# Three bf16 attentions of a transformer stack rewritten as float32r flows whose operands are laid out by DMA

## The chip, the cores and the metric

The kernel runs on one core of one Trainium2 chip, as one launch. The metric is the device time of that launch in microseconds (us). The engines are named as the profile names them: PE is TensorE (its weight loads are listed apart as PEld), DVE is VectorE, ACT is ScalarE, POOL is GpSimd, and SP is SyncE, which here issues nearly all DMA transfers.

## The reference, cut to what matters

Eight sub-layers follow each other on an activation of shape (8, 256, 128), each added to it through a tanh gate:

```python
x = x + jnp.tanh(g_xattn[0]) * _L0_xattn_ref(_layernorm(x), ctx_1024, ctx_1024)
x = x + jnp.tanh(g_ffn[0])   * _L0_ffn_ref(_layernorm(x), ...)
x = x + jnp.tanh(g_xattn[1]) * _L1_xattn_ref(...)
x = x + jnp.tanh(g_ffn[1])   * _L1_ffn_ref(...)
x = x + jnp.tanh(g_xattn[2]) * _L2_xattn_ref(_layernorm(x), ctx_1024, ctx_1024, W, b, mask)
x = x + jnp.tanh(g_ffn[2])   * _L2_ffn_ref(...)
x = x + jnp.tanh(g_xattn[3]) * _L3_xattn_ref(...)
x = x + jnp.tanh(g_ffn[3])   * _L3_ffn_ref(...)
```

The change touches four attentions. Three have 16 heads of 8 channels over 8 sequences of 256 queries and 256 keys: L0's (rotary, causal), L2's (causal, with a padding mask) and L3's (with four projections, not causal). The fourth lies in L0's feed-forward: a chain of six nodes, each with an attention of 8 heads of 16 channels over the same 8 sequences, 48 attentions in all, here called L0f. Each is `softmax(q k^T * scale) v` in float32.

## The kernel before, in words

**Precision.** A float32 value is too fine for one fast matmul pass, so each operand is cut into parts. The three small-head attentions use class `Heads`: POOL (`att_pool`, lines 359 to 400) cuts each of q and k into three bf16 parts and writes six products' worth of them side by side (six times 8 columns for each head), so that a contraction over 48 rows gives the product in full. L0f uses class `Flow`: two parts (high and low) in float32r, three products, 48 rows for its heads of 16 channels.

**Small-head flow (`att_pool`, `att_pe`, `att_act`, `att_dve`).** One unit is one sequence: 16 heads, worked in 8 pairs. PE turns the stacked bf16 parts by transposes (events K and T, 16 of 128x128 each; line 434). ACT copies the turned q out of PSUM (552), DVE the turned k (566). Pass A (476) gives the scores with queries on the rows; DVE takes each row's maximum from them (573, 574, or 576 where not causal), writes its negative into the stack (586, 588), and PE turns the q stack once more with this row in it (event X, 16 transposes; ACT copies it at 556). Pass B (489) computes the scores again with keys on the rows and the maximum already subtracted. ACT takes the exponential (548), V (503) multiplies by the values with a column of ones that yields the denominator, O (543) copies the sum out, R (513) turns it back, and DVE divides (598, 601). In the causal layers two groups of four mask matmuls (444 and 453) come before A and B of each pair.

**L0f's flow (`flow_*`).** One unit is one node and sequence: 8 heads, 4 pairs. Matmuls with the node's weights (event S, line 952) already leave q and k transposed in PSUM. ACT writes the high parts to `Z` (1049), DVE the low parts (event L, 1097). Then SP copies, from SBUF to SBUF, six pieces of 128 KB into `QK` (event D, line 876), each piece spreading one pair of parts into every third row of a slot. `QK` is a ring of three units. The negated maxima are turned by PE (event N, 979), negated by DVE into `NMrow` (1091), and SP copies them as one row into the slots (866). Pass B (990) of the first two pairs waits for the first such copy, of the last two for the second.

**Order.** Every engine walks the same list, `events()`, and executes its own kinds in that order. Software pipelining is in that list: in one step, pass B of one unit runs with pass A of the next, while units further on are prepared. SP walks it too, in order, so a DMA behind a waiting DMA waits with it. PE executes in order; A of a pair waits until DVE has taken the maxima of the pair before (one set of PSUM banks), B until ACT has taken the exponential of the pair before.

**Around it.** Each stage begins and ends with a barrier of all five engines (line 259 is that wait in the profile). Before a small-head flow POOL clears the two stacks and V (350 to 356) and does stage work: in L0 it rotates k, in L2 it turns the padding mask into numbers (1791). Before L0f's flow POOL blanks the ring (1159).

Of the kernel before, what the change touches and what calls it, by code (L numbers as in the profile page):

```python
# [8 lines left out]
F32 = mybir.dt.float32  # L9
# [12 lines left out]
PARTS = 6  # L22
MASKED = -1.0e30
ROUND = 12582912.0
Q_SLOTS = ((0, 3), (3, 2), (5, 1))


class Heads:


    def __init__(self, dh, causal):
        self.dh, self.causal = dh, causal
        self.H = D // dh
        self.halves = self.H // 8
        self.units = 8
        self.per = self.H // self.units
        self.cols = P // self.per
        self.pad = PARTS * dh
        self.top = self.pad + 1
        self.end = self.pad + 3  # L40
        self.scale = float(dh) ** -0.5
        self.pairs = self.H // 2

    def events(self):

        pairs, last = self.pairs, self.halves - 1
        out = [("K", 0, 0), ("K", 0, 1), ("T", 0, 0), ("T", 0, 1)]
        for s in range(B + 1):  # L50
            a, b, more = s < B, s >= 1, s + 1 < B
            for j in range(pairs):
                if j == pairs - 1 and more:
                    out += [("K", s + 1, 0), ("K", s + 1, 1)]
                if a:
                    out.append(("A", s, j))
                if j < pairs - 1 and b:
                    out.append(("B", s - 1, j + 1))
                elif j == pairs - 1 and a:
                    out.append(("B", s, 0))  # L60
                if b and j % 2 == 1:
                    out.append(("V", s - 1, j // 2))
                    if j % 4 == 3:
                        out.append(("O", s - 1, j // 4))
                if b and j == 0:
                    out.append(("X", s - 1, 1))
                if a and j == pairs // 2:
                    out.append(("X", s, 0))
                if j == 1 and s >= 2:
                    out.append(("R", s - 2, last))  # L70
                if b and last and j == 5:
                    out.append(("R", s - 1, 0))
                if j == pairs - 2 and more:
                    out += [("T", s + 1, 0), ("T", s + 1, 1)]
        return out + [("R", B - 1, last)]


class Flow:
# [6 lines left out]
    def __init__(self, dh, causal, units, node):  # L85
        self.dh, self.causal, self.units, self.node = dh, causal, units, node
# [6 lines left out]
        self.scale = float(dh) ** -0.5  # L93

# [10 lines left out]
    def events(self):  # L105
# [10 lines left out]
        for s in range(-3, self.units + 1):  # L116
            z, w, a, b, f = s + 3, s + 2, s + 1, s, s - 1
            for j in range(self.pairs):
                if ok(b):
                    out.append(("B", b, j))  # L120
                if ok(a):
                    out.append(("A", a, j))
                if j == 2 and ok(z):
                    out.append(("L", z, 0))
                if j == 0 and ok(b):
                    out.append(("N", b, 1))
                if j == half and ok(a):
# [15 lines left out]
                if j == 1 and ok(z):  # L143
                    out.append(("S", z, 0))
# [12 lines left out]
def flamingo(nc, T, out):  # L157
    with ExitStack() as ctx:
# [30 lines left out]
        Mx = sb("Mx", [P, 2, 16])  # L189
        Rden = sb("Rden", [P, 2, 16])  # L190
# [6 lines left out]
        sh = ExitStack()  # L197
        Qst = sb("Qst", [P, 2, 2, 8, P], BF16, scope=sh)
        Kst = sb("Kst", [P, 2, 8, P], BF16, scope=sh)
        QT = sb("QT", [P, 2, 8, S], BF16, scope=sh)  # L200
        KT = sb("KT", [P, 2, 8, S], BF16, scope=sh)
        QpT = sb("QpT", [P, 8, S], BF16, scope=sh)
# [5 lines left out]
        rope = sb("rope", [P, 2, 2, 4], scope=s0)  # L208
        s0.close()
# [5 lines left out]
        padi = sb("padi", [P, NT], I32, scope=s4)  # L215
        padf = sb("padf", [P, NT], scope=s4)
        s4.close()
        sh.close()
# [8 lines left out]
        q_split, k_split = sem("q_split"), sem("k_split")  # L227
        tpT_full, tpT_free = sem("tpT_full"), sem("tpT_free")
        tpK_full, tpK_free = sem("tpK_full"), sem("tpK_free")
        tpX_full, tpX_free = sem("tpX_full"), sem("tpX_free")  # L230
        sm_full, max_done, max_in = sem("sm_full"), sem("max_done"), sem("max_in")
# [108 lines left out]
        def stack(ap, L):  # L340

            return ap.rearrange("p t u (g c) -> p (t u g) c", g=L.per)

# [3 lines left out]
        def stack_fill(g, L, pad_bias=None):  # L347

            e = g.eng
            g.link(e.memset(Qst[:], 0.0))  # L350
            g.link(e.memset(Kst[:], 0.0))
            g.link(e.memset(V[:, 0:NT * L.H * 32], 0.0))
            g.link(e.memset(v_view(L)[:, :, :, L.dh:L.dh + 1], 1.0))
            for t in range(2):
                g.link(e.memset(stack(Qst[:, t], L)[:, :, L.pad:L.pad + 1], 1.0))
            g.link(e.memset(stack(Kst[:], L)[:, :, L.top:L.end], 1.0))
# [2058 lines left out]
```

## Time and profile before

| what | value |
|---|---|
| median of 3 runs | 2091.3 us (2089.96 to 2099.73) |
| the profiled execution | 2090.75 us |
| its span, first to last instruction | 2088.8 us |
| mean granted clock of TensorE | 0.857 of full |
| busy: PE, DVE, ACT, POOL | 1383.4, 1399.1, 806.9, 448.6 us |
| flow of L0's attention, about | 52 to 218 us |
| L0f's flow, about | 263 to 774 us |
| flow of L2's attention, about | 1325 to 1489 us |
| flow of L3's attention, about | 1608 to 1779 us |

A row of a timeline reads: start in us, duration in us, engine, line, operation, written and read tile, shapes, count, and in brackets how long the engine had been idle and what ended that. A row of a group reads: busy us, mean ns of one, then the idle time in front of the group and its cause. Matmul durations contain a pipeline latency of about 0.17 us, so four matmuls that follow each other overlap in the rows; the start of the next group tells how long they occupy PE.

### The profile page before, as it was taken

How to read it: one execution, taken by the hardware profiler on the slowest of the kernel's cores; microseconds unless marked ns; L12 is line 12 of the kernel's file. 1: busy time of each engine (PE TensorE's matmuls, PEld its weight loads, DVE VectorE, ACT ScalarE, POOL GpSimd, SP SyncE). 2: the span in 40 equal slices, each digit the busy share in tenths (PEclk: the TensorE clock that was granted, in tenths of full speed). 3: DMA queues.
4: the chain of work that ended last, by engine and by line, in shares of the span. 5: the costliest groups of instructions: out<-in, count | busy, mean ns of one | idle time of the engine just before them, and what ended most of it. 6: DMA issues, size and time to landing. Idle time of an engine off the chain costs nothing. (4 is left out here: it accounts for less than half of the span.)

```text
span 2088.8 us, 34728 instructions
## 1 busy us (share of the span) xinstructions
PE 1383.4 (66%) x13753; PEld 966.7 (46%) x13754; DVE 1399.1 (67%) x2126; ACT 806.9 (39%) x1151; POOL 448.6 (21%) x596
## 2 busy tenths in 40 slices
PE   0788168888888870788888833388523677140898
PEld 0565146566656640465665521266413344120797
DVE  5565446676667758577677768566586676859565
ACT  0466136666666650333333311266320477010110
POOL 6431332222222101122222200532003331000221
PEclk9999569999999995999999965599856699655798
DMA  2011322233222311000000000000000000110242
GB/s 66 3 9 10 91 64 78 79 86 79 78 78 80 90 32 62 1 1 1 1 1 1 1 11 12 12 2 2 11 0 30 1 2 2 59 20 0 86 131 94
DMA packets 97736, 76.51 MB, mean 37 GB/s; under 512 B 42612, under 2 KB 84148, under 8 KB 96692
## 3 DMA queue, kind: packets, MB, share of 16 engines
q1 hardware_dynamic: 96564, 73.10, 12.8%
q8 instruction: 107, 1.75, 0.4%
q0 software_dynamic: 1024, 1.32, 0.3%
q14 instruction: 41, 0.34, 0.1%
HBM read 33.10 MB, written 3.15 MB: 17 GB/s over the span
## 5 line engine op out<-in xcount | busy, mean ns | idle before, releaser
L1086 DVE TENSOR_REDUCE Mf<-bank 128x4 f32<-128x1024 f32 x192 | 234.5, 1221 | 148.6 <-PE bank L972 148.4
L1039 ACT ACTIVATE Pt<-bank 128x1024 f32<-128x1024 f32 x192 | 196.8, 1025 | 83.5 <-PE bank L990 82.8
L548 ACT ACTIVATE Pt<-bank 128x768 f32<-128x768 f32 (+1 forms) x192 | 169.4, 882 | 135.4 <-PE bank L489 134.5
L1312 POOL TENSOR_TENSOR Psum<-Pt 128x512 f32<-128x512 f32 x64 | 81.1, 1267 | 315.3 <-ACT Pt L1431 315.3
L990 PE MATMUL bank<-QK 50*128 50x256 f32 x768 | 98.9, 336 | 51.0 <-DMA QK<-NMrow 50.0
L758 PE MATMUL bank<-ident,Qf 128*128 128x128 f32 x64 | 14.3, 416 | 156.9 <-SPq L259 94.5
L1479 DVE RECIPROCAL st<-bank 128x256 f32<-128x256 f32 x64 | 111.9, 1748 | 6.9 <-PE bank L1392 6.8
L896 POOL CAST parts<-nodes 128x256 fp32r<-128x256 f32 x96 | 38.2, 397 | 339.1 <-PE bank L952 339.1
L1454 DVE TENSOR_TENSOR qk_lo<-bank,qk_hi 128x512 fp32r<-128x512 f32 x64 | 44.1, 689 | 97.1 <-ACT qk_hi L1423 97.1
L990 PEld LDWEIGHTS bank<-QK 50*128 50x128 f32 x768 | 58.8, 190 | 106.9 <-DMA QK<-NMrow 59.2
L573 DVE TENSOR_REDUCE Mx<-bank 128x2 f32<-128x256 f32 x128 | 54.3, 424 | 80.5 <-PE bank L476 76.4
L1003 PE MATMUL bank<-Pt,V 128*32 128x256 f32 x1536 | 107.8, 400 | 0.1
L1431 ACT ACTIVATE Pt<-bank 128x1024 f32<-128x1024 f32 x64 | 65.5, 1024 | 77.8 <-PE bank L1375 77.8
L503 PE MATMUL bank<-Pt,V 128*32 128x256 f32 (+1 forms) x1536 | 91.7, 357 | 2.9 <-ACT Pt L548 2.9
L476 PE MATMUL bank<-KT,QT 49*128 49x256 bf16 (+1 forms) x768 | 73.6, 273 | 30.0 <-DVE Mx L576 26.6
L576 DVE TENSOR_REDUCE Mx<-bank 128x4 f32<-128x1024 f32 x64 | 78.2, 1221 | 21.9 <-PE bank L476 21.8
L1968 POOL DMA_INDIRECT xg<-s_rows,sloti x32 | 29.3, 916 | 293.0 <-PEq L259 201.1
L972 PE MATMUL bank<-QK 49*128 49x256 f32 x768 | 81.9, 292 | 12.1 <-DMA QK<-Z 6.8
L574 DVE TENSOR_REDUCE Mx<-bank 128x2 f32<-128x512 f32 x128 | 87.0, 680 | 0.0
L758 PEld LDWEIGHTS bank<-ident,Qf 128*128 128x128 f32 x64 | 12.9, 224 | 157.7 <-SPq L259 95.0
L434 PE MATMUL bank<-identb,Kst 128*128 128x128 bf16 x384 | 33.0, 241 | 76.8 <-POOL Kst L387 69.0
L1387 PE MATMUL bank<-Pt,V 128*64 128x256 f32 x512 | 70.2, 395 | 19.5 <-DVE AnT L1481 19.5
(367 smaller groups left out, 3687.6 us busy)
## 6 DMA issues: line engine op xcount, KB each, us to landing
QK<-Z SPq DMA_DIRECT2D x288, 128.0 KB, 3.3
Wup<-in_L_upT SPq DMA_DIRECT2D x16, 512.0 KB, 3.5
Wdn<-in_L_downT SPq DMA_DIRECT2D x16, 256.0 KB, 3.7
Aup<-in_L_aupT SPq DMA_DIRECT2D x16, 128.0 KB, 3.5
QK<-NMrow SPq DMA_DIRECT2D x96, 4.0 KB
WeT<-in_L_WeT SPq DMA_DIRECT2D x1, 1280.0 KB
s_rows<-XG SPq DMA_DIRECT2D x1, 1032.0 KB, 8.2
tA<-in_x_heads SPq DMA_DIRECT2D x1, 1024.0 KB
```

What stands on the lines that cost most here:

```text
L476: last = pe.matmul(bank[x][:, t * S:t * S + w], QT[rs, n % 2, u, t * P:(t + 1) * P], KT[rs, n % 2, u, 0:w], start=(not L.causal and t == 0 ...
L503: last = pe.matmul(bank[4][32 * x:32 * x + 32, c + q0:c + S], Va[:, 2 * n + k, 4 * i + x, :], Pp[:, (f + x // 2) % 4, x % 2, k * S:k * S + ...
L548: act.activation(Pp[:, g % 4, :, 0:w], banks[:, 2:4, 0:w], ACT.Exp, scale=L.scale).then_inc(exp_done, 1)
L574: d.tensor_reduce(Mx[:, 1, hs], banks[:, 0:2, S:2 * S], AX, ALU.max).then_inc(max_done, 1)
L576: d.tensor_reduce(Mx[:, :, hs].rearrange("p t h -> p h t"), banks[:, 0:2, :].rearrange("p h (t k) -> p h t k", t=2), AX, ALU.max).then_inc ...
L972: last = pe.matmul(bank[x][:, t * S:(t + 1) * S], QK[rs, u % 3, k, 0, t * P:(t + 1) * P], QK[rs, u % 3, k, 1, :], start=(t == 0), stop=Tru ...
L990: last = pe.matmul(bank[2 + x][:, t * S:(t + 1) * S], QK[rs, u % 3, k, 1, t * P:(t + 1) * P], QK[rs, u % 3, k, 0, :], start=(t == 0), stop ...
L1003: last = pe.matmul(bank[4][32 * x:32 * x + 32, S * (j % 2):S * (j % 2) + S], Va[:, 2 * n + k, 4 * j + x, :], Pp[:, (f + x // 2) % 4, x % 2 ...
L1039: act.activation(Pp[:, g % 4], banks[:, 2:4, :], ACT.Exp, scale=L.scale).then_inc(exp_done, 1)
L1086: d.tensor_reduce(m, banks[:, 0:2, :].rearrange("p h (t k) -> p h t k", t=2), AX, ALU.max).then_inc(max_done, 1)
L1312: e.tensor_tensor(Psum[:, q % 2], Pp[:, q % 4, :, 0:S], Pp[:, q % 4, :, S:2 * S], ALU.add).then_inc(key_sum, 1)
L1479: d.reciprocal(st1[:], y[:, S:2 * S]).then_inc(pair_done, 1)
```

## The change

`Heads` and `att_*` go; all four attentions are `Flow`s. What is different for the three with 8 channels:

- Two float32r parts instead of three bf16 ones: 24 rows of products, one for the mask and one for the maximum, in slots of 32 rows, four heads to a column block of 128 rows.
- POOL only reorders columns: four copies of 128x128 to a unit (event S). PE turns them with 4 float32 transposes, ACT copies the high parts (128x512), DVE subtracts for the low parts (128x512).
- SP lays the parts into the slots: per unit 12 copies of 64 KB (events D, 0 to 3, three copies each), in L2 a 13th with the padding mask. Two small copies per unit bring the maxima.
- In a step, A stands ahead of B, as before in the causal layers. D stands at pairs 1, 2, 3 and 5, the maxima (N) at pairs 0 and 4, S at pair 7, L at pair 0. R is at pairs 1 and 5, V at pairs 0, 2, 4 and 6.
- The masks stay as they were, bf16, four matmuls each. The short matmuls of the causal layers (128 columns) become float32r too.
- POOL clears only V, then blanks the ring with six casts of 128x1024; in L2 the mask is now handled as 16 x 2048 numbers rather than 128 x 16. SP also stores L0's output rows from within the flow, at event R.

For L0f:

- the ring holds four units instead of three, so blanking takes eight casts instead of six;
- the six copies of a unit go in two lots of three: the first at pair 3 of the step in which its parts are made, the second at pair 1 of the next step. Before, all six stood at pair 0 of the next step.

The core of the diff:

```diff
-        self.copies = 3 * self.per
+        self.copies = 3 * self.per + padded
+        self.ring = 4 if node else 3
...
             for j in range(self.pairs):
-                if ok(b):
+                if ok(b) and self.node:
                     out.append(("B", b, j))
                 if ok(a):
                     out.append(("A", a, j))
-                if j == 2 and ok(z):
+                if ok(b) and not self.node:
+                    out.append(("B", b, j))
+                if self.node and j == 2 and ok(z):
                     out.append(("L", z, 0))
+                elif not self.node and j == 0 and ok(w):
+                    out.append(("L", w, 0))
...
-                if j == 0 and ok(w):
-                    out.append(("D", w, 0))
+                if self.node and j == 3 and ok(z):
+                    out.append(("D", z, 0))
+                elif self.node and j == 1 and ok(w):
+                    out.append(("D", w, 1))
+                elif not self.node and j in (1, 2, 3, 5) and ok(w):
+                    out.append(("D", w, j - 1 - j // 5))
...
-                if j == 1 and ok(z):
+                if j == (1 if self.node else self.pairs - 1) and ok(z):
                     out.append(("S", z, 0))
...
+        def slots_blank(g, L):
+            for r in range(L.ring):
+                for k in range(2):
+                    g.eng.tensor_copy(L.QK[:, r, :, k, :], bc(L.rowk[:, k:k + 1].unsqueeze(1), [P, 4, S]))
...
+                elif kind == "R" and rows_out and j == L.outs - 1:
+                    rows_out(u)
                 elif kind == "D":
-                    e.wait_ge(stk_done, u + 1)
-                    if u >= 3:
-                        e.wait_ge(st_full, base["P"] + L.pairs * (u - 2))
-                    for r in range(L.per):
-                        rows = slice(L.slot * r, L.slot * r + 4 * L.dh)
+                    e.wait_ge(L.stk_done, u + 1)
+                    if u >= L.ring:
+                        e.wait_ge(st_full, base["P"] + L.pairs * (u - L.ring + 1))
+                    if L.padded and j == 0:
+                        e.dma_start(L.QK[L.pad:P:L.slot, u % L.ring, :, 1, :].bitcast(F32),
+                                    padr[:, u, :].bitcast(F32)).then_inc(L.slots_in[u % L.ring], 16)
+                    rows = slice(L.slot * j, L.slot * j + 4 * L.dh)
+                    for f, pick in enumerate((slice(1, 3), slice(1, 4, 2), slice(0, 3, 2))):
...
+                if kind == "S" and not L.node:
+                    for k, src in enumerate((Qf, Kf)):
+                        for t in range(2):
+                            e.tensor_copy(L.permuted(L.order[:, u % 2, k, t, :], out=True),
+                                          L.permuted(src[:, 2 * u + t, :])).then_inc(L.parts_in, 1)
...
+                    else:
+                        last = act.copy(L.Z[:, u % 2, 1:3, :].rearrange("p k s -> p (k s)"), b)
...
+                    else:
+                        last = d.tensor_tensor(L.Z[:, u % 2, 0:4:3, :], b.rearrange("p (k s) -> p k s", k=2),
+                                               L.Z[:, u % 2, 1:3, :].bitcast(F32), ALU.subtract)
...
-                (wx[:, 3], T["L2_WT"]), (bx[:, 3], row_bc("L2_xattn_b", D)), (padi[:], T["pad_cols"])]
+                        (padi[:], T["mask_BxS2_if0"].unsqueeze(0).to_broadcast([16, B, S])),
...
-                g.link(g.eng.tensor_scalar(padf[:], padi[:], 1.0, MASKED, ALU.is_equal, ALU.mult))
+                g.link(g.eng.tensor_scalar(padr[:], padi[:], 1.0, MASKED, ALU.is_equal, ALU.mult))
```

## Rows read from the trace of the kernel before

**Rows 1.** Stretch of L0f's flow: busy PE, PEld, DVE, ACT, POOL; clock, DMA.

```profile
277.00:770.00 493.00, 427.03 (x4258) 292.59 (x4258) 331.62 (x504) 312.96 (x483) 100.22 (x186) 0.96 0.29 77
```

**Rows 2.** Timeline of L0's small-head flow, one pair to the next.

```profile
143.41 0.40 PE L444 MATMUL bank<-cmask,identb 128*128 128x128 bf16 x4 [0.40 <-DVE Mx L574]
...
143.96 0.34 PE L476 MATMUL bank<-KT,QT 49*128 49x128 bf16 x4
...
144.39 0.86 PE L503 MATMUL bank<-Pt,V 128*32 128x256 f32 x16
...
144.68 0.68 DVE L574 TENSOR_REDUCE Mx<-bank 128x2 f32<-128x512 f32 x1
...
145.68 0.39 PE L444 MATMUL bank<-cmask,identb 128*128 128x128 bf16 x4
```

**Rows 3.** The same timeline, mask of the pair after.

```profile
148.99 0.39 PE L444 MATMUL bank<-cmask,identb 128*128 128x128 bf16 x4
```

**Rows 4.** Groups by line and shape; then two rows of L0f's timeline.

```profile
L972 PEld LDWEIGHTS bank<-QK 49*128 49x128 f32 x768 | 61.7, 194 | 15.5 <-DMA QK<-Z 7.8 <-issue 3.9 <-DVE Mf L1086 3.2
L961 PE MATMUL bank<-Kf,nodes 128*128 128x128 f32 x192 | 30.3, 282 | 0.0
L476 PEld LDWEIGHTS bank<-KT,QT 49*128 49x128 bf16 x768 | 22.6, 96 | 63.1 <-DVE Mx L576 33.6 <-issue 13.5 <-ACT QT L552 3.6
...
504.82 0.51 PE L990 MATMUL bank<-QK 50*128 50x256 f32 x4
...
505.16 0.40 PE L972 MATMUL bank<-QK 49*128 49x256 f32 x4
```

**Rows 5.** Waits of PE in L0f; then the timeline around two `NMrow` copies.

```profile
PE bank L990 <- DMA QK<-NMrow: 50.0, 44, 2.4
...
285.56 5.13 SPq L866 DMA_DIRECT2D QK<-NMrow  x2
...
287.32 0.79 PE L990 MATMUL bank<-QK 50*128 50x256 f32 x4 [0.89 <-DMA QK<-NMrow]
...
510.10 5.36 SPq L866 DMA_DIRECT2D QK<-NMrow  x2
...
512.55 0.50 PE L990 MATMUL bank<-QK 50*128 50x256 f32 x4 [1.14 <-DMA QK<-NMrow]
```

**Rows 6.** Timeline of two flow starts: L0's small heads, then L0f.

```profile
51.69 0.40 POOL L378 CAST Kst<-Kf 128x256 bf16<-128x256 f32 x1 [8.16 <-DVEq L259]
...
60.92 0.50 PE L476 MATMUL bank<-KT,QT 49*128 49x128 bf16 x4 [0.79 <-ACT QT L552]
...
267.40 2.93 PE L952 MATMUL bank<-parts,wst 128*128 128x256 f32 x12 [2.13 <-DVE bv L1125]
...
270.92 7.84 SPq L876 DMA_DIRECT2D QK<-Z  x12
...
277.94 0.80 PE L972 MATMUL bank<-QK 49*128 49x256 f32 x4 [6.76 <-DMA QK<-Z]
```

**Rows 7.** POOL: three groups, then its timeline in L2 and L3.

```profile
L350 POOL MEMSET Qst<- 128x4096 bf16 x3 | 10.5, 3512 | 54.0 <-DVEq L259 54.0
L1159 POOL CAST QK<-rowk 128x1024 fp32r<-128x1024 f32 x6 | 7.5, 1294 | 8.2 <-DMA V<-in_L_ffn_We 8.2
L886 POOL COPY Kf<-V 128x128 f32<-128x128 f32 x12 | 4.5, 404 | 4.8 <-PEq L259 4.8
...
1324.37 0.32 POOL L1791 TENSOR_SCALAR padf<-padi 128x16 f32<-128x16 int32 x1 [7.01 <-issue]
...
1616.43 0.66 POOL L380 TENSOR_TENSOR rest<-Kf,Kst 128x256 f32<-128x256 f32 x1 [7.80 <-issue]
```

**Rows 8.** L3's maxima: their group; one unit apart on the timeline.

```profile
L576 DVE TENSOR_REDUCE Mx<-bank 128x4 f32<-128x1024 f32 x64 | 78.2, 1221 | 21.9 <-PE bank L476 21.8
...
1697.56 0.60 DVE L586 TENSOR_SCALAR Qst<-Mx 128x16 bf16<-128x16 f32 x1
...
1714.83 0.60 DVE L586 TENSOR_SCALAR Qst<-Mx 128x16 bf16<-128x16 f32 x1
```

More of the change, by code:

```diff
@@ L21, with __init__ @@
 NT = B * S // P
-PARTS = 6
 MASKED = -1.0e30
 ROUND = 12582912.0
[L25 to L75, printed above, removed]
 class Flow:
-    def __init__(self, dh, causal, units, node):
-        self.dh, self.causal, self.units, self.node = dh, causal, units, node
+    def __init__(self, name, dh, causal, units, node=False, padded=False):
+        self.name, self.dh, self.causal, self.units = name, dh, causal, units
+        self.node, self.padded = node, padded
         self.H = D // dh
@@ L208, in flamingo @@
         rope = sb("rope", [P, 2, 2, 4], scope=s0)
+        L0.hold(sb, s0)
         s0.close()
@@ L471, in att_pe @@
                         pe.wait_ge(max_done, g)
                     for t in range(2):
-                        w = P if (L.causal and t == 0) else S
+                        w = P if L.causal and t == 0 else S
                         for x in range(2):
-                            rs, u = rows(2 * i + x, L.pad + 1)
-                            last = pe.matmul(bank[x][:, t * S:t * S + w], QT[rs, n % 2, u, t * P:(t + 1) * P],
-                                             KT[rs, n % 2, u, 0:w], start=(not L.causal and t == 0),
+                            rs, k = L.rows(2 * j + x, L.top)
+                            last = pe.matmul(bank[x][:, t * S:t * S + w],
+                                             L.QK[rs, u % L.ring, k, 0, t * P:(t + 1) * P],
+                                             L.QK[rs, u % L.ring, k, 1, 0:w], start=(not L.causal and t == 0),
@@ L484, in att_pe @@
                         pe.wait_ge(exp_done, g)
                     for t in range(2):
-                        q0 = P if (L.causal and t == 1) else 0
+                        q0 = P if L.causal and t == 1 else 0
                         for x in range(2):
-                            rs, u = rows(2 * i + x, L.end)
-                            last = pe.matmul(bank[2 + x][:, t * S:t * S + S - q0], KT[rs, n % 2, u, t * P:(t + 1) * P],
-                                             QpT[rs, u, q0:S], start=(not L.causal and t == 0), stop=True,
-                                             skip_group_check=True)
+                            rs, k = L.rows(2 * j + x, L.top + 1)
+                            last = pe.matmul(bank[2 + x][:, t * S:t * S + S - q0],
+                                             L.QK[rs, u % L.ring, k, 1, t * P:(t + 1) * P],
+                                             L.QK[rs, u % L.ring, k, 0, q0:S], start=(not L.causal and t == 0),
+                                             stop=True, skip_group_check=True)
@@ L500, in att_pe @@
+                    o = Ub + L.outs * u + j // 2
+                    if j % 2 == 0 and o > 0:
+                        pe.wait_ge(ot_free, o)
                     for k in range(2):
-                        q0 = P if (L.causal and k == 1) else 0
+                        q0 = P if L.causal and k == 1 else 0
+                        o = S * (j % 2)
                         for x in range(4):
-                            last = pe.matmul(bank[4][32 * x:32 * x + 32, c + q0:c + S], Va[:, 2 * n + k, 4 * i + x, :],
+                            last = pe.matmul(bank[4][32 * x:32 * x + 32, o + q0:o + S], Va[:, 2 * n + k, 4 * j + x, :],
@@ L529, in turn_bank @@
[L529 to L544 removed]
+                    b = turning(kind, u, j)
@@ new lines, in flow_pe @@
+                    pe.wait_ge(norm_done, 2 * (Ub + u + 1))
+                    for t in range(2):
+                        last = pe.transpose(b[:, t * P:(t + 1) * P], O[:, 2 * n + t, :], ident[:, :])
+                    last.then_inc(t_full, 1)
+                elif kind == "U":
+                    b = turning(kind, u, j)
+                    pe.matmul(b[:, 0:S], WeS[:, c, :], nodes[:, c, cols], start=True, stop=False)
+                    pe.wait_ge(t_done, u + 1)
+                    pe.matmul(b[:, 0:S], Wn[:, 3, c, :], attT[:, u % 2, :], start=False, stop=True).then_inc(u_full, 1)
```

774 lines of the change are left out of this document (291 added, 483 removed).

## The prediction

> **What bounds the kernel now.** I first split the span into stages and ask each flow what ends last in it. In L0f's flow, 493 us long, PE is busy 427.03 us at a granted clock of 0.96 (nearly all of it at 2.4 GHz) and every other engine less [rows 1]. PE runs almost back to back there, except for one wait: the table of waits gives 50.0 us in 44 times to the copy of `NMrow` [rows 5]. That is where L0f can be shortened. The small-head flows are bound by a loop, not by a busy engine: mask matmuls, pass A, the maxima on DVE, the next masks. In rows 2 the mask starts at 143.41, A 0.55 later, and DVE's second reduction ends at 144.68 + 0.68 = 145.36; with 0.06 for the signal the next mask could start at 145.42, a turn of 2.01 us. It started at 145.68, so this turn took 2.27: V and the turning of the sums (R) were still in PE's queue. The turn after it takes 148.99 − 145.68 = 3.31 [rows 2, 3], since the 32 transposes of K and T and their copies are in it. A unit is eight turns: five of 2.01, two of 2.27 and one of 3.31 make 17.9 us. L3, without masks, takes 1714.83 − 1697.56 = 17.27 a unit [rows 8].
>
> **Part 1, L0f's copies in two lots.** Of a row copy issued when nothing else is under way, the reader starts 287.32 − 285.56 = 1.76 us later; of one issued right behind six 128 KB copies, 512.55 − 510.10 = 2.45 us later [rows 5]. I take the difference, 0.69 us, as the price of standing behind them. After the change three copies leave after the second row copy of a step and three after the first, so the row copy at pair 2 follows only three copies that ended some 2.3 us earlier, and the one at pair 0 three that ended about 2 us earlier. I take 1.76 for both: 44 × 0.69 = 30 us less over the 48 units. Ends: nothing, if what is late is the copy's own latency; 50 us if the whole wait goes. What is late next is PE itself, at 87% of this stretch. Blanking takes two more casts, of 1.29 us on average and less where DVE doesn't disturb them [rows 7]; POOL is the last engine at that barrier, so nothing hides them: +2. L0f: −28.
>
> **Part 2, start of a small-head flow.** Before, the first A begins 60.92 − 51.69 = 9.2 us after POOL starts [rows 6]. Now: POOL's four reorderings 4 × 0.40 = 1.6 [rows 7]; then transposes, ACT's and DVE's copies, which in L0f took 270.92 − 267.40 = 3.5 from PE's start to the first DMA [rows 6], with more matmuls, so 3.0 here. SP's 12 issues took 7.84, or 0.65 each [rows 6], so the last starts 7.2 after the first. From the start of the sixth issue (270.92 + 5 × 0.65) to the A that waits for it is 277.94 − 274.17 = 3.8; for pieces of half the size I take 3.0. Sum 14.8, or +5.6; POOL's reorderings overlap a little, so I take +5, in L2 +5.6 with the 13th copy. Bounds: +3 (all but the issues a third shorter) and +9 (a piece that takes twice as long to land).
>
> **Part 3, a turn of the causal flows.** A float32r weight load is 194 ns on average, a bf16 one 96 [rows 4], and it stands open between the masks and A: +0.09. Four float32r matmuls of 256 columns occupy PE 505.16 − 504.82 = 0.34 [rows 4]; two by two, at 2.4 GHz, they would stream in 0.21, so 0.13 of each group is weight load, of which I take +0.11 as new. No row shows a float32r matmul of 128 columns. Low end: it streams at the rate of 256 columns, +0. High end: as plain float32 of 128 columns, 282 ns, about 0.11 of it beyond the 0.17 of latency, where bf16 takes half: +0.05 per group [rows 4]. That row has its size and word width, so I take it. The loop grows to 2.01 + 0.09 + 0.05, and 0.03 for the second weight load, 2.18. PE's own work in a turn with V: mask to A 0.55 + 0.09; A and B 0.43 up to V [rows 2] + 2 × 0.16; V 0.8 (its 0.86 less the tail): 2.19, with N 0.2 more. A unit: 8 × 2.18 + 0.45 = 17.9. What the longer turns take, the 48 transposes that go give back; the four big copies that ACT loses lay beside the loop. Steady pace: no change, from −0.5 (low end) to +1.4 a unit (a turn 0.2 longer, V slots bound by PE). Seven units with A and B together: −4 to +10 in each of L0 and L2. The eight turns with A alone, at half clock, and the last eight with B alone carry the same additions: 8 × 0.17 + 8 × 0.12 = +2.3.
>
> **Part 4, POOL before the flows.** It loses two fills, 3.5 [rows 7] and half of that, and gains six casts (7.5, with one stalled), about +1. In L0 DVE was last (POOL had waited 8.16 us at the end [rows 6]), so +0.5 for the later DMA. In L2 POOL is the last too: +1, and the mask conversion, 16 numbers in 0.32 before, becomes 2048 in a row; a cast of 1024 takes 1.29, so 2.3 more; casts beside DVE's long layer norm add another 1.2. L2: +4.5, from 0 to +9. The stall of 7.01 in front of it stays [rows 7]. In L3 the stall of 7.80 stood in front of POOL's first TENSOR_TENSOR after a barrier that had everything else waiting [rows 7]; now POOL has only copies and casts there, before which no row shows such a stall: −7.8.
>
> The Trainium skill (GPSIMD Engine Reference, Instruction dispatch) says that the first call of a freshly loaded kernel costs some 6 us more. The two stalls of 7.0 and 7.8 agree in size; both come behind a partition reduction. If that rule held for copies as well, the first cast or fill would pay it; in L2 that would be under the layer norm and give 7 us back, in L3 it would change nothing, and the sum would be 7 less.
>
> **Part 5, L3's pace.** DVE needs 1.22 for a maximum [rows 8]; a turn is A 0.45, DVE 1.22, 0.06: 1.74. PE with V: 0.34 + 0.34 + 0.2 + about 1.07 (0.86 and the columns that the causal layers leave out), 1.95, and with N 2.3; DVE at pair 0 also has the low parts and a row, 2.4. The unit: 2.4 + 1.9 + 1.95 + 1.74 + 2.3 + 1.9 + 1.95 + 1.74 = 15.9, −1.4 against 17.27 [rows 8], ×7 = −9.6. Flows start at half clock (four matmuls of A take 0.80 in rows 6, 0.40 in rows 4), and there V fills a turn alone, so I take −8. Start: +5 of part 2, −7.8 of part 4, ends +1.8. L3: −9, from −22 to +2.
>
> **Sum.** L0: 0.5 + 5 + 2.3 + 0 = +8. L0f: −28. L2: 4.5 + 5.6 + 2.3 = +12.4. L3: −9. Together −16.6 on the profiled execution's 2090.75 (span 2088.8 and 1.95 around it), which lies 0.6 below the median of 2091.3. So 2074, −0.8%. Half a percent (10.5 us) is about what can be told from no change.
>
> The Trainium skill (DMA: Bandwidth & Descriptors, Why a DMA increments its semaphore by 16 and not by 1) says that a copy is spread over the largest number of engines up to 16 that divides the outermost sizes of both sides. By it a piece that ends in 8 rows runs on 8 engines, where L0f's of 16 rows had 16; it would occupy them as long as the old ones did theirs. A DMA share of 0.29 [rows 1] of some 10 us a unit is 2.9 us for six copies, or 0.48 a piece, under the 0.65 of an issue, and the sum stays; the rule makes the rival of the copies below possible. No row here shows how many engines a copy had.
>
> **Rivals.**
> (a) L0f's wait does not move: the row copy needs 2.4 us whatever stands before it, because its end must be signalled behind all data of its queue. For it: the wait is there in 44 of 48 units [rows 5]. Against it: 1.76 at the flow's start [rows 5], though at a time when PE ran at half clock. The small heads then stand alone: 2074 + 28 = 2102, slower than before. It decides from 17 us of lost gain. Chance 0.14.
> (b) Causal turns cost more: short float32r matmuls are dearer than plain float32, or the PE queue with A, B, V and N is longer than the loop. For it: my sum for a V turn is already at 2.19 of 2.18. 14 units × 1.4 = +20: 2094, no change. Chance 0.20.
> (c) The wait in L0f goes altogether, and L2's stall hides: 2074 − 20 − 7, about 2047 to 2055. For it: shortening the chain also lets DVE start earlier. Chance 0.16.
> (d) The slot copies bound the small heads: 12 copies a unit, SP occupied 12 × 0.65 + two rows + two stores, 10.3 of 17.9. It decides from 1.4 us a copy; at 1.6 a unit takes 20, and 14 × 2.1 + 7 × 4.1 = 58 more give 2132. Against it: L0f moves as many bytes in 10 us [rows 1]. Chance 0.07.
> The forecast itself has 0.43, with 2062 to 2086.
>
> **The numbers.** Faster by over 0.5% (under 2080): most of the forecast, all of (c), a little of (b): 0.57. Within: most of (b), the rest of the forecast, some of (a): 0.25. Slower: most of (a), (d), tail of (b): 0.18. Range 2048 to 2101, which leaves out (d) and half of (a) above and the best of (c) below; the likeliest case's own is 2062 to 2086.
>
> **What would show it.** In the changed trace: PE's wait for `NMrow` in L0f near 20 us instead of 50, and units some 0.6 us shorter; between POOL's first reordering and the first A about 14.8 us, three times; turns of 2.18 in the causal flows, and the float32r matmuls of 128 columns near 282 ns; POOL's stall still in L2, none in L3; L3's units near 16. It is wrong if a unit of the causal flows is over 19 us, or if L0f's stretch stays at 493 us.

## The result, and the profile after

| | before | after |
|---|---|---|
| median | 2095.5 us (4 runs) | 2217.4 us (4 runs, 2195.0 to 2228.9) |
| ratio | | 1.0548, 95% interval 1.0454 to 1.0641: slower |
| profiled execution, span | 2088.8 us | 2193.1 us |
| mean granted clock of TensorE | 0.857 | 0.792 |
| busy: PE, DVE, ACT, POOL | 1383.4, 1399.1, 806.9, 448.6 us | 1505.3, 1379.5, 732.5, 364.0 us |

The slowest run of the changed kernel, 2228.9 us, lies over 1.5% above its fastest and is not in the ratio; the other three have a median of 2211.6 us, and every difference from the changed kernel below is counted from that. The forecast of 2074 was wrong by 143 us (138 from 2211.6), outside its range and on the other side. DVE, ACT and POOL have less to do than before; PE is busy 122 us longer though 48 transposes a unit are gone. To see where, I cut both spans at marks that both kernels have: DVE's negated row maxima in L0f (96 of them), and POOL's first instruction in L2's and in L3's flow. Of a tile's row the columns are the duration (ns, minimum/median/maximum), then the first and last start; under it stand rows of the timeline. Before:

```profile
L1091 DVE TENSOR_SCALAR NMrow<-bank x96: 401/402/412, 285.1 to 763.0; 4x256 fp32r<-4x256 f32 x96
```

```profile
1324.87 0.40 POOL L378 CAST Kst<-Kf 128x256 bf16<-128x256 f32 x1 [0.19 <-SPq L259]
...
1607.67 0.40 POOL L378 CAST Kst<-Kf 128x256 bf16<-128x256 f32 x1 [20.53 <-SPq L259]
```

After, with POOL's two other rows that matter for the starts:

```profile
L638 DVE TENSOR_SCALAR l0f_NMrow<-bank x96: 401/402/411, 327.6 to 765.3; 4x256 fp32r<-4x256 f32 x96
```

```profile
34.76 1.03 POOL L730 TENSOR_TENSOR tB<-ctxS,rope 128x512 f32<-128x512 f32 x1 [7.56 <-issue]
...
1328.07 7.13 POOL L1576 TENSOR_SCALAR padr<-padi 16x2048 fp32r<-16x2048 int32 x1 [7.32 <-issue]
1335.39 0.73 POOL L376 COPY l2x_order<-Qf 128x128 f32<-128x128 f32 x2 [0.19 <-POOLq L236]
...
1673.42 0.73 POOL L376 COPY l2x_order<-Qf 128x128 f32<-128x128 f32 x2 [21.12 <-DVEq L236]
```

| stretch | before | after | after − before |
|---|---|---|---|
| start to L0f's first row (with L0's flow) | 285.1 | 327.6 | +42.5 |
| L0f, first to last row | 477.9 | 437.7 | −40.2 |
| to POOL's start in L2 | 561.9 | 570.1 | +8.2 |
| L2's start to L3's start | 282.8 | 338.0 | +55.2 |
| L3's start to the end | 481.1 | 519.7 | +38.6 |

L0f gained more than forecast, and the three small-head flows lost about 33 (L0), 51 (L2) and 48 us (L3) beside what was counted for them. Why is in the stretches of L2's and L3's flow. The columns are the stretch and its length, busy us (and instructions) of PE, PEld, DVE, ACT and POOL, the granted clock, the DMA share and GB/s. Before, L2 in full pace, then L3:

```profile
1400.00:1475.00 75.00, 64.22 (x1033) 45.88 (x1030) 49.31 (x110) 46.73 (x58) 17.96 (x30) 1.00 0.01 2
1680.00:1763.00 83.00, 62.38 (x872) 36.62 (x872) 65.16 (x88) 61.95 (x68) 21.23 (x34) 1.00 0.01 1
```

After, L2, then L3, then for comparison L0f:

```profile
1400.00:1450.00 50.00, 44.39 (x526) 31.74 (x524) 25.59 (x57) 20.59 (x28) 2.87 (x8) 0.84 0.13 46
1450.00:1500.00 50.00, 48.39 (x390) 35.18 (x390) 19.68 (x43) 15.08 (x20) 0.00 (x0) 0.50 0.10 34
1705.00:1882.00 177.00, 163.20 (x1117) 93.82 (x1118) 86.03 (x110) 80.05 (x88) 5.54 (x16) 0.50 0.08 28
360.00:770.00 410.00, 380.80 (x3958) 263.55 (x3958) 305.34 (x464) 290.25 (x449) 90.81 (x168) 1.00 0.31 84
```

The clock column is the finding: 0.50, the lower of TensorE's two levels (1.2 GHz), through all of L3's flow and parts of L2's, with PE busy 163.20 / 177 = 92% of L3's stretch; before, 1.00 with PE busy 75 to 86%. So it was not want of busy time that kept the engine at half clock; since at half rate the same work fills more of the time, the comparison that decides is e2's, below, with the same instructions. The durations say the same: a causal group of A takes 0.49 us at full rate and 0.79 at half. (In L0 the column prints 1.00 where A takes 0.79; there the durations count.) The timeline shows one such fall in L2. From 1440 to 1447 us PE was busy 5.55 of 7 us (79%) at a clock of 1.00, and its longest pause was 0.95 us. Pass A, turn by turn, and the rows around the fall:

```profile
1444.72 0.49 PE L502 MATMUL bank<-l2x_QK 25*128 25x128 f32 x4
...
1446.34 0.40 PE L431 MATMUL bank<-cmask,identb 128*128 128x128 bf16 x4 [0.95 <-DVE l2x_Mf L631]
...
1446.89 0.49 PE L502 MATMUL bank<-l2x_QK 25*128 25x128 f32 x4
...
1447.82 1.40 PE L542 MATMUL bank<-Pt,V 128*32 128x256 f32 x16
1449.14 0.61 PE L431 MATMUL bank<-cmask,identb 128*128 128x128 bf16 x4
...
1450.11 0.79 PE L502 MATMUL bank<-l2x_QK 25*128 25x128 f32 x4
...
1453.05 0.79 PE L502 MATMUL bank<-l2x_QK 25*128 25x128 f32 x4
```

A turn of 2.17 us becomes one of 2.9 to 3.5, and up to 4.0 with PE transposes in it. A causal unit takes 17.6 us at full clock (A from 147.70 to 165.31 in L0) and 26.5 at half (1450.11 to 1476.65 in L2); L3's takes 21.8 at half (1712.37 to 1734.20). There A, B and V leave PE hardly a pause; V's group takes 1.94 us where before it took 1.07:

```profile
1736.32 0.79 PE L502 MATMUL bank<-l2x_QK 25*128 25x256 f32 x4 [0.90 <-DVE l2x_Mf L633]
...
1737.98 1.94 PE L542 MATMUL bank<-Pt,V 128*32 128x256 f32 x16
```

### The profile page after: what moved, and what is told of

It reads as the page before. It is cut to its first block and busy times, and to the rows that moved or that the text cites. A ratio compares the mean times of both kernels' runs of the same rounds, so it can differ in the third digit from the quotient of the medians.

```text
span 2193.1 us, 32944 instructions
## 1 busy us (share of the span) xinstructions
PE 1505.3 (69%) x12794; PEld 1048.0 (48%) x12794; DVE 1379.5 (63%) x2054; ACT 732.5 (33%) x1079; POOL 364.0 (17%) x476
## 5 line engine op out<-in xcount | busy, mean ns | idle before, releaser
L578 ACT ACTIVATE Pt<-bank 128x1024 f32<-128x1024 f32 (+1 forms) x384 | 366.0, 953 | 310.3 <-PE bank L525 309.6
L633 DVE TENSOR_REDUCE l0f_Mf<-bank 128x4 f32<-128x1024 f32 x192 | 234.5, 1221 | 108.8 <-PE bank L502 108.8
L542 PE MATMUL bank<-Pt,V 128*32 128x256 f32 (+1 forms) x3072 | 242.7, 445 | 3.0 <-ACT Pt L578 2.9
L542 PEld LDWEIGHTS bank<-Pt,V 128*32 128x32 f32 x3072 | 92.2, 126 | 97.4 <-issue 67.3
L633 DVE TENSOR_REDUCE l2x_Mf<-bank 128x4 f32<-128x1024 f32 x64 | 78.5, 1226 | 80.6 <-PE bank L502 78.7
L820 PE MATMUL bank<-ident,Qf 128*128 128x128 f32 x64 | 14.7, 424 | 163.3 <-SPq L236 96.5
L502 PE MATMUL bank<-l2x_QK 25*128 25x256 f32 (+1 forms) x512 | 94.8, 464 | 28.3 <-DVE l2x_Mf L633 17.6
L525 PE MATMUL bank<-l0f_QK 50*128 50x256 f32 x768 | 97.8, 333 | 19.6 <-DMA l0f_QK<-l0f_NMrow 18.8
L431 PE MATMUL bank<-cmask,identb 128*128 128x128 bf16 x512 | 66.2, 271 | 63.7 <-DVE l0x_Mf L631 20.5
L1208 ACT ACTIVATE Pt<-bank 128x1024 f32<-128x1024 f32 x64 | 65.5, 1024 | 76.2 <-PE bank L1152 76.2
L502 PE MATMUL bank<-l0f_QK 49*128 49x256 f32 x768 | 79.7, 286 | 12.6 <-DMA l0f_QK<-l0f_Z 7.4
L431 PEld LDWEIGHTS bank<-cmask,identb 128*128 128x128 bf16 x512 | 38.2, 116 | 98.0 <-DVE l0x_Mf L631 30.4
```

Source lines behind the costliest of these rows:

```text
L431: pe.matmul(bank[x][:, o:o + P], identb[:, :], cmask[:, 0, :], start=(t == 0), stop=False, skip_group_check=True)
L502: last = pe.matmul(bank[x][:, t * S:t * S + w], L.QK[rs, u % L.ring, k, 0, t * P:(t + 1) * P], L.QK[rs, u % L.ring, k, 1, 0:w], start=(not ...
L525: last = pe.matmul(bank[2 + x][:, t * S:t * S + S - q0], L.QK[rs, u % L.ring, k, 1, t * P:(t + 1) * P], L.QK[rs, u % L.ring, k, 0, q0:S], ...
L542: last = pe.matmul(bank[4][32 * x:32 * x + 32, o + q0:o + S], Va[:, 2 * n + k, 4 * j + x, :], Pp[:, (f + x // 2) % 4, x % 2, k * S:k * S + ...
L578: act.activation(Pp[:, g % 4, :, 0:w], banks[:, 2:4, 0:w], ACT.Exp, scale=L.scale).then_inc(exp_done, 1)
L633: d.tensor_reduce(m, banks[:, 0:2, :].rearrange("p h (t k) -> p h t k", t=2), AX, ALU.max).then_inc(max_done, 1)
```

## The experiments

Two theories stood once the traces were compared. C: with 25 rows in A and B and without the transposes the array has too little to do, and its clock falls though PE is busy. W: the flows are slower by added work and waits, and the clock is low for a reason of its own, such as the pause at a flow's start (later called P).

**L0f's part alone** (e1), on the kernel before:

```
-        QK = sb("QK", [P, 3, 4, 2, S], F32R, scope=s1)
+        QK = sb("QK", [P, 4, 4, 2, S], F32R, scope=s1)
-                if j == 0 and ok(w):
-                    out.append(("D", w, 0))
+                if j == 3 and ok(z):
+                    out.append(("D", z, 0))
+                elif j == 1 and ok(w):
+                    out.append(("D", w, 1))
```

> The kernel before with L0f's part of the change alone: its slot ring of four units and its copies in two lots of three; the three small-head attentions stay as they were. All theories here say that this part is the one that worked: in the trace of the changed kernel its flow took 437.6 us between the first and last row-copy issue instead of 478, so 40 us less, and +2 us for two more blanking casts: about 2053 to 2057. If the gain in L0f came instead from something around it (another state of the clock or of the queues after the new L0), it would stay at 2085 or more.

Measured: 2055.6 us, ratio 0.9836 (0.9784 to 0.9888), 40 us less than the 2095.3 beside it. PE's wait for `NMrow` is 18.6 us. This part works by itself.

**Ring of four, but one lot** (e10), against e1:

```
-                if j == 3 and ok(z):
-                    out.append(("D", z, 0))
-                elif j == 1 and ok(w):
-                    out.append(("D", w, 1))
+                if j == 0 and ok(w):
+                    out += [("D", w, 0), ("D", w, 1)]
```

> The kernel before with L0f's ring of four units, but all six copies in one lot behind the row copy as before (two more blanking casts, no other difference). If what the row copy waits for is the three to six copies issued ahead of it, the ring alone gives nothing: 2095 to 2098, PE's wait for NMrow 50 us in 44. If the ring's freedom is what frees the row copy, it comes down to 2056 as with both.

Measured: 2094.9 us, ratio 0.9997 (0.9975 to 1.0018), and the wait is whole. The waits of PE (us in all, times, longest) in e10, in e1 and in the changed kernel:

```profile
PE bank L990 <- DMA QK<-NMrow: 50.9, 46, 2.2
```

```profile
PE bank L992 <- DMA QK<-NMrow: 18.6, 45, 0.9
```

```profile
PE bank L525 <- DMA l0f_QK<-l0f_NMrow: 18.8, 44, 0.9
```

The ring alone gives nothing; what stands ahead of the row copy is what it waits for. Two lots in a ring of three were not run.

**64 rows in A and B** (e2), on the changed kernel's small heads (A's edit; B's is alike):

```
-  rs, k = L.rows(2 * j + x, L.top)
+  rs, k = slice(64 * x, 64 * x + 64), L.rows(2 * j + x, 1)[1]
```

> The changed kernel, with passes A and B of the small heads contracting over 64 rows each (two heads' slots together) in place of 25 or 26: the same number of matmuls, of columns and of waits, only more rows of the array at work; it leaves out the separation of the two heads, so its scores are sums over two heads. Theory C (the loss in the small-head flows is TensorE's clock, which rows at half rate show, and what the array has to do is too little to bring it up): the clock comes up, units of the causal flows fall from 21.6 to 26.6 us to near 17.6 and L3's from 21.8 to near 16; three flows of some 35 to 40 us too much come back in large part: 2217 - 80 to 110 = 2107 to 2137. Theory W (the loss is added work and waits in the turn, and the clock is low for reasons of its own, such as the pause at the flow's start): no change, 2205 to 2225.

Measured: 2086.4 us, ratio 0.9954 (0.9925 to 0.9983), 125 us less than the changed kernel, with the same instructions; that is below even the 2107 to 2137 that C gave. Windows of L2 and L3, then A and V in L3's timeline:

```profile
1400.00:1450.00 50.00, 42.74 (x586) 30.83 (x586) 29.44 (x66) 22.98 (x31) 1.43 (x4) 1.00 0.13 46
1720.00:1760.00 40.00, 30.67 (x364) 17.82 (x366) 24.60 (x34) 25.93 (x28) 0.00 (x0) 1.00 0.06 22
```

```profile
1700.52 0.51 PE L502 MATMUL bank<-l2x_QK 64*128 64x256 f32 x4 [0.33 <-DVE l2x_Mf L633]
1701.19 1.07 PE L542 MATMUL bank<-Pt,V 128*32 128x256 f32 x16
```

The clock is 1.00, and PE is less busy (77% in L3's window) than where it was 0.50. C holds, W falls. The flows of e2 still begin at half rate: in L0, A takes 0.79 or 0.80 us from 71.64 to 97.55, eleven turns, and 0.50 from then on; the changed kernel stays at 0.79 until 143.84. L3's unit, by POOL's reorderings 1673.04 and 1688.43, is 15.4 us.

**48 bf16 matmuls a unit added** (e3), written to a turning bank before S (16), N (8 each) and R (8 each):

```
+  def fill(b, times):
+      for k in range(times):
+          pe.matmul(b[:, (k % 4) * P:(k % 4 + 1) * P], identb[:, :],
+                    cmask[:, 0, :], start=True, stop=True)
```

> The changed kernel with 48 added bf16 matmuls of 128 x 128 columns per small-head unit, written to a turning bank ahead of the transposes that overwrite them (16 at S, 8 at each N, 8 at each R): about the PE work that the removed transposes were. Theory C: the clock comes up; at full clock the 48 cost PE some 48 x 0.1 = 5 us at half and 2.6 us at full clock a unit, partly beside the loop; units of 18 to 19 us instead of 21.6 to 26.6; the whole at 2217 - 50 to 90 = 2127 to 2167. Theory W: PE only gets more to do in a turn it fills already; 24 units x 2.6 to 5 us = 60 to 120 us more: 2280 to 2330.

Measured: 2155.2 us, ratio 1.029 (1.0237 to 1.0342): 56 us less time with more work. The clock comes back in part, 0.93 in L2's full pace:

```profile
1400.00:1450.00 50.00, 47.34 (x651) 36.06 (x649) 26.53 (x58) 20.66 (x28) 4.34 (x12) 0.93 0.11 39
```

**L0f's part undone in the changed kernel** (e4):

```
-        self.ring = 4 if node else 3
+        self.ring = 3
-                if self.node and j == 3 and ok(z):
-                    out.append(("D", z, 0))
-                elif self.node and j == 1 and ok(w):
-                    out.append(("D", w, 1))
+                if self.node and j == 0 and ok(w):
+                    out += [("D", w, 0), ("D", w, 1)]
```

> The changed kernel with L0f's part undone: ring of three, all six copies of a unit in one lot behind the row copy; the small heads stay changed. If the two parts add, it takes what L0f gains: 2217 + 38 to 42 = 2255 to 2259, and PE's wait for NMrow in L0f is 50 us again. If the small heads' part is what slows through L0f (its gain depends on what stands before), it differs by 20 us or more from that.

Measured: 2276.4 us, ratio 1.0898 (1.0837 to 1.096): 65 more than the changed kernel, not 40. L0f's stretch of rows takes 498.4 us (342.5 to 840.9), PE's wait for the row copy 62.9 us in 46. In its flow the 128 KB copies land in 3.7 us (median) where the kernel before has 3.3, and take 38.2% of the engines' time instead of 28.5%, for as many bytes (28.8 and 28.6 MB in windows of 390 and 370 us). So the two parts do not simply add; why these copies are slower was not found.

**The rows and the transposes in the old kernel** (e5, e6, e7): all bf16, in the old order, without slot copies.

```
e5:  -  rows(2 * i + x, L.pad + 1)        +  rows(2 * i + x, 25)
     -  rows(2 * i + x, L.end)            +  rows(2 * i + x, 26)
e6:  -  pe.transpose(..., src(u), identb[:, :])
     +  pe.matmul(..., src(u)[0:16], identb[0:16, :], start=True, stop=True)
e7:  both
```

> The kernel before, its small heads' passes A and B contracting over 25 and 26 rows in place of 49 and 51; all else, the 48 bf16 transposes a unit too, as it was. It leaves out half of each head's parts in the scores. Instructions, columns and waits are the same. Theory C1 (the rows of A and B carry the clock by themselves): TensorE falls back to half rate in the small-head flows as in the changed kernel, and three flows take up to 35 us more each: 2150 to 2200. Theory C2 (rows and transposes together carry it; either one left is enough, as most of the clock came back with 48 added matmuls): 2090 to 2110. Theory W (no matter of rows): 2095.

> The kernel before, where the 48 transposes a unit of the small heads read 16 of the 128 rows (as matmuls of the same 128 columns, so PE streams as long as before); A and B keep 49 and 51 rows. It leaves out seven eighths of what is transposed, so the scores are of other numbers. C1: no change, 2095. C2: no change or little, 2095 to 2110. If the transposes alone carried the clock: 2150 or more.

> The kernel before with both edits of the two runs beside it: 25 and 26 rows in A and B, 16 rows in the transposes; every instruction, column and wait as before, and still bf16. It leaves out what those leave out. C1 and C2: half rate in the small-head flows and 2150 to 2200, which would show the loss without any of the changed kernel's float32r, copies or new order. Theory W: 2095.

| | rows of A, B | rows of the transposes | median | ratio (95%) |
|---|---|---|---|---|
| before | 49, 51 | 128 | 2091.8 | |
| e5 | 25, 26 | 128 | 2105.6 | 1.0081 (1.0051 to 1.0111) |
| e6 | 49, 51 | 16 | 2114.5 | 1.0106 (1.0078 to 1.0134) |
| e7 | 25, 26 | 16 | 2171.2 | 1.0390 (1.0363 to 1.0418) |

L3's flow in e5, e6 and e7; before, this stretch has the clock at 1.00:

```profile
1680.00:1763.00 83.00, 67.16 (x822) 39.49 (x819) 60.78 (x83) 58.13 (x64) 20.46 (x32) 0.88 0.01 1
```

```profile
1680.00:1763.00 83.00, 71.12 (x836) 38.32 (x836) 61.93 (x82) 58.43 (x65) 25.15 (x40) 0.84 0.01 1
```

```profile
1680.00:1763.00 83.00, 78.67 (x680) 44.41 (x674) 50.37 (x67) 47.53 (x52) 19.71 (x32) 0.54 0.01 1
```

Each reduction alone costs 14 and 23 us, both together 79. That is C2 with a small loss for each (e6 lies 5 us above its range): the old kernel, without float32r, copies or new order, loses clock when both are taken from it. The clock falls most in L3; in L2 (1400 to 1475) e7's clock is 0.91. This carries more than half, not all, of the loss: 79 of what e2 gives back, 125.

The edits on the rows of A and B (e5 against before, e7 against e6, e2 against the changed kernel) change nothing else in the instructions, though the values that pass through the array change too. The edit on the transposes changes more than rows: it puts ordinary matmuls, written as float32, in place of TensorE's transposes. Both stream as long (16 of q's at half rate take 1.89 us before and 1.88 in e6), but no run parts the 16 rows from the change of operation.

**A warm start** (e8, e12): 100 and 170 of e3's matmuls on PE ahead of each flow's first A, and no others.

```
+                    if j == 0 and u == 0 and not L.node:
+                        fill(bank[0], 100)        # e12: 170
                     if j == 0:
                         pe.wait_ge(L.slots_in[u % L.ring], ...)
```

> The changed kernel with 100 bf16 matmuls of 128 columns on PE ahead of each small-head flow's first A, into that pass's bank, while PE waits for the slot copies anyway (10.99 us in L0). If the pause at the start is what keeps the clock down (theory P), units run at full rate from the first on, and the three flows come near those with 64 rows: 2217 - 90 = 2110 to 2140. If a clock that is up falls again with 25 rows (C1, C2), the first unit or two gain 2 to 5 us each and the rest is as slow as before: 2190 to 2220.

> The changed kernel with 170 bf16 matmuls of 128 columns ahead of each small-head flow's first A in place of the 100 of the run before this: those 100 took 6.91 us, mostly at full rate, but ended 4.22 us before the copies landed, and the first A was at half rate (0.79 us). Now PE has next to no pause. If a pause is what brings the clock down (theory P), the first A takes 0.49 to 0.50 us and the flows stay at full rate: 2110 to 2140. If too few rows at work bring it down with PE busy (theory C), the flow starts at full rate and falls to half within the eight turns of A alone, or at the latest in the unit after: 2190 to 2220.

Measured: 2213.5 us (ratio 1.0554, 1.048 to 1.0629) and 2199.5 us (1.0506, 1.0463 to 1.0549). L0's start in e12:

```profile
59.93 10.19 PE L447 MATMUL bank<-cmask,identb 128*128 128x128 bf16 x170
71.06 0.40 PE L431 MATMUL bank<-cmask,identb 128*128 128x128 bf16 x4 [0.94 <-DMA l0x_QK<-l0x_Z]
71.39 0.49 PE L511 MATMUL bank<-l0x_QK 25*128 25x128 f32 x4
73.00 0.40 PE L431 MATMUL bank<-cmask,identb 128*128 128x128 bf16 x4 [1.12 <-DVE l0x_Mf L640]
73.33 0.49 PE L511 MATMUL bank<-l0x_QK 25*128 25x128 f32 x4
74.95 0.61 PE L431 MATMUL bank<-cmask,identb 128*128 128x128 bf16 x4 [1.12 <-DVE l0x_Mf L640]
75.49 0.79 PE L511 MATMUL bank<-l0x_QK 25*128 25x128 f32 x4
```

The flow starts at full rate, A in 0.49, and falls in the third turn, to 0.79; it is back at 0.50 only at 146.5 us. PE is busy little there (1.35 of the 3.6 us from 71.4 to 75.0, with A alone), so this fall by itself does not tell few rows from little work. It does show that the pause at a flow's start is not the cause: without it the kernel is hardly faster (2199.5 against 2211.6 us), and L3's flow falls in its third turn too (A 0.50 at 1695.61, 0.79 at 1697.43) and stays down. The Trainium skill (TensorE: Matmul & The Clock Gate, HAM oscillation — how this bites in real kernels) gives the rule "no PE-idle gaps" and tells of falls behind waits for DMA. No run here contradicts that a pause costs the clock, but the fall at about 1448 us in L2 came behind seven microseconds of which PE was busy 79%, with 0.95 us as the longest pause, and e2 holds full clock through L3 with PE busy 77% and pauses of up to 1.21 us, so the rule is not enough.

**POOL's work ahead of the flows** (e9), with e2's 64 rows as a base: rotation before blanking in L0; in L2 the mask on ACT.

```
-  g.eng.tensor_scalar(padr[:], padi[:], 1.0, MASKED, ALU.is_equal, ALU.mult)
+  a.eng.activation(padr[:], padi[:], ACT.Copy, scale=MASKED)
```

> The kernel with 64 rows in the small heads' passes (two heads' slots together, so that their scores are sums over two heads), and in it two edits on POOL's work ahead of the flows: in L0 the rotation of K comes before the six blanking casts instead of after them, and in L2 the padding mask is converted by ACT (idle there) instead of POOL. If the extra time ahead of the flows is POOL's 7.13 us conversion and its rotation beside DVE's, L2's flow starts 7 us and L0's 4 to 5 us earlier: 2086 - 12 = 2074, which is where the sum of the prediction stood for a chip at full clock. If POOL's stall of 7 us moves into the place of what is removed, it stays at 2083 to 2087.

Measured: 2077.4 us, ratio 0.9924 (0.9895 to 0.9953), 9.0 less than e2, which the intervals alone don't resolve; the stretch does. From L0f's last row (742.4) to L2's start (1305.49) it takes 563.1 us, 8.7 less than in e2 (571.8). With the mask went POOL's stall in front of it: 6.96 and 7.13 us in e2. POOL now waits 5.74 us for DVE there, so not all of it shows. On ACT the mask takes 1.89. L0 gained nothing (flow from 56.02 instead of 56.22): the stall moved with the rotation, 7.47 in front of it, and the six casts beside DVE, which is last at that barrier, slowed it as much.

```profile
1297.53 1.89 ACT L1600 ACTIVATE padr<-padi 16x2048 fp32r<-16x2048 int32 x1
...
26.86 1.03 POOL L730 TENSOR_TENSOR tB<-ctxS,rope 128x512 f32<-128x512 f32 x1 [7.47 <-issue]
```

**The fastest version measured** (e11): e1 and one tiny multiplication on POOL ahead of L3.

```
                 g.eng.drain().then_inc(v_blank, 1)
+                g.link(g.eng.tensor_tensor(rest[:, 0:1], rest[:, 1:2],
+                                           rest[:, 2:3], ALU.mult))
```

> The kernel before with L0f's part of the change (ring of four, two lots) and one multiplication of 128 x 1 on POOL in the 20.5 us that it idles before L3's flow. If POOL's stall of 7.80 us in L3 falls on the first operation of its kind after what stands before, wherever that is, it is hidden there: 2056 - 7.8 = 2048. If the stall belongs to the place (behind the barrier), it stays and the time is 2056.

Measured: 2052.2 us, ratio 0.979 (0.9768 to 0.9811). It beats both kernels. The stall moved to where POOL idled, and the flow's own multiplication has none:

```profile
1560.23 0.18 POOL L1796 TENSOR_TENSOR rest<-rest 128x1 f32<-128x1 f32 x1 [7.11 <-issue]
1574.68 0.40 POOL L380 CAST Kst<-Kf 128x256 bf16<-128x256 f32 x1 [14.27 <-SPq L261]
1575.03 0.61 POOL L381 CAST Kst<-Kf 128x512 bf16<-128x512 f32 x1
1575.72 0.67 POOL L382 TENSOR_TENSOR rest<-Kf,Kst 128x256 f32<-128x256 f32 x1
```

From L3's start to the end it takes 475.1 us instead of e1's 481.3. The medians differ by 3.4 us, which their intervals don't resolve.

## Why the prediction was wrong

The step that failed is "steady pace: no change" in part 3, and the pace of part 5. Both took the full clock of the old flows (0.55 from mask to A, 0.34 a group) as given, and credited the 48 transposes as pure saving; that A and B contract over half as many rows was given no effect. No term and no rival asked what keeps the clock up once they are gone; the sentence on half clock covered the starts alone. The mark set beforehand, a causal unit over 19 us, was passed (from one of POOL's reorderings to the next, 116.57 to 143.12 in L0 and 1370.34 to 1396.05 in L2: 26.5 and 25.7).

Since e2 is the changed kernel with its clock kept but for the starts of the flows, it prices the other terms; what the clock took is the rest.

| | forecast | with the clock kept (e2 − before) | the clock's share (after − e2) |
|---|---|---|---|
| start to L0f's first row | +8, +2 for blanking | +19.5 | +23.0 |
| L0f | −30 | −40.2 | 0 |
| L2, start and flow | +12.4 | +9.9 + 12.8 = +22.7 | −1.7 + 42.4 |
| L3 | −9 | −5.2 | +43.8 |
| sum | −16.6 | −3.2 | +107.5 |

The last column is taken between two profiled executions; by the medians it is 125. Without the fall the forecast would have been 13 us too low in sum: L0f's gain was 10 us larger, and each of the small-head flows cost more than its term. In L0, part of that is the clock again: eleven turns at half rate where the kernel before had eight. Step by step:

- **L0f, part 1: right in kind, too small.** The wait fell by 31 us (50.0 [rows 5] to 18.8), as forecast; the flow gained 40. Some of the rest is the clock: 0.98 before (320 to 763 us), 1.00 after (360 to 765). In e10, at 1.00 too, the rows take 472.8 us, and in e1 437.1: 35.7 less, of which the wait is 32.3. Rival (a) fell, and e10 shows that the ring alone does not do it.
- **Start, part 2: right.** Between POOL's first reordering and the first A: 71.78 − 56.30 = 15.5, 15.9 in L2 (with the thirteenth copy) and 1688.08 − 1673.42 = 14.7 in L3, against 14.8; before it was 9.2 in L0 [rows 6].
- **A turn, part 3: right in sum where the clock is full, partly by luck.** L0 after, one pair to the next; 2.17 us against 2.18:

```profile
151.49 0.40 PE L431 MATMUL bank<-cmask,identb 128*128 128x128 bf16 x4
...
152.04 0.49 PE L502 MATMUL bank<-l0x_QK 25*128 25x128 f32 x4
152.38 0.35 PE L525 MATMUL bank<-l0x_QK 26*128 26x256 f32 x4
153.66 0.40 PE L431 MATMUL bank<-cmask,identb 128*128 128x128 bf16 x4 [0.94 <-DVE l0x_Mf L631]
```

  The terms came out otherwise. From mask to A it takes 0.55 as before, not 0.09 more; A's own group lasts 0.49 instead of 0.34 [rows 2], 0.15 more where 0.08 was taken. The two misses nearly cancelled. A unit in e2 takes 124.70 − 107.08 = 17.6, between the normalisations of two units, against 17.9; before it is 110.37 − 92.47 = 17.9. Rival (b) fell. The end cost 2.8 instead of 1 (from the normalisation before the last unit's to its own: 213.11 to 233.60 in e2, 199.87 to 217.57 before).
- **POOL ahead of the flows, part 4: half right.** The stall is gone in L3 and stays in L2, and casts and copies have none, as forecast; the Trainium skill's extra cost for the first call of a freshly loaded kernel (GPSIMD Engine Reference, Instruction dispatch) did not fall on the first cast; a stall in L0 that no partition reduction stands before also speaks against the link to one. Two things were missed. L0 got a stall it did not have, 7.56 in front of its rotation, which put that beside DVE's (DVE's 128x512 multiplications took 1.41 instead of 0.69), and the flow started 4.6 us later instead of 0.5. The mask took 7.13, not 2.3 more than 0.32 [rows 7], and from POOL's first fill (1301.35; before 1301.58) to the flow's start it took 34.0 instead of 23.3: 10.8 more, not 4.5, and above the bound of 9.
- **L3, part 5: right at full clock only (e2).** 15.4 us a unit against 15.9, and 17.27 before [rows 8]; 21.8 in the changed kernel.
- **Rivals (c) and (d)** did not come: 18.8 us of L0f's wait are left, and PE waits for slot copies only at the flows' starts.

What stays open: why the clock came back in the middle of L0's and L2's flow and not in L3's; how much of the loss goes to the rows of A and how much to B's; whether it is the rows of the transposes or the operation that counts; and why L0f's copies occupy the DMA engines longer in e4. The spread of the changed kernel, 34 us over four runs, fits falls at different places, but that was not traced.

## What to carry to other kernels

Where small matmuls carry a stage, the transposes beside them and the rows that they contract over may be what keeps TensorE at full clock: before counting their removal as a gain, ask what the array does without them, and price the stage at half clock as a rival. In a trace, read the granted clock beside the busy share, since at half clock PE only looks like the bound. And when a copy is late, look first at what was issued ahead of it: splitting the lot in a ring of four gave 40 us, the deeper ring alone nothing.

## What the runs showed of the hardware

- TensorE stayed at half clock with PE busy 92% (L3 after) and 97% (1450 to 1500 in L2 after), and at full clock with PE busy 77% (L3 in e2). Between the two kernels the instructions are the same; the number of contracted rows differs, 25 and 26 against 64, and with it the values. It is not float32r: in bf16 (e7) the clock fell to 0.54 in L3 too.
- A float32r group of two matmuls of 128 and two of 256 columns occupied PE 152.38 − 152.04 = 0.34 us in pass A, as long as four of 256 [rows 4]. The short ones saved nothing there. In pass B the same mix took 0.27 (L2 after, 1447.23 to 1447.50).
- POOL's stall of about 7 us stood before a multiplication or another arithmetic operation and never before copies, casts or fills: 7.56, 7.47, 7.32 and 7.11 in four places. Not every stage has one: the old L0's first multiplication (27.34 us) waited 0.32. What decides that was not found. In e11 an operation of 128 x 1 took it as well as a large one, so it could be put where POOL idles.
- POOL's conversion of 16 x 2048 int32 took 7.13 us, ACT's 1.89.
